# A one-core Flamingo layer stack: the matmul fillers of the slot passes and the last stage left out

## What is computed

```python
x = x + tanh(g_xattn[0]) * L0_xattn(layernorm(x), ctx, ctx, mask)
x = x + tanh(g_ffn[0])   * L0_ffn(layernorm(x))          # relu MLP, 512 wide
x = x + tanh(g_xattn[1]) * L1_xattn(layernorm(x), ctx, ctx)   # one key head
x = x + tanh(g_ffn[1])   * L1_ffn(layernorm(x))          # 16 experts, top 2, and a shared one
x = x + tanh(g_xattn[2]) * L2_xattn(layernorm(x), ctx, ctx)
x = x + tanh(g_ffn[2])   * L2_ffn(layernorm(x))          # 32 experts, top 1
x = x + tanh(g_xattn[3]) * L3_xattn(layernorm(x), ctx)   # slot attention
x = x + tanh(g_ffn[3])   * L3_ffn(layernorm(x), rhs)     # int8 product
```

```python
for _ in range(3):                                   # the slot passes
    q = rmsnorm(slots) @ Wq
    attn = softmax(q @ k.T * scale, axis=slots)      # over the slots
    attn = attn / (attn.sum(axis=keys) + eps)
    slots = gru_cell(attn @ v, slots)                # r, z, n gates
```

## Time and profile before

| | |
|---|---|
| median of 3 runs | 342.53 us (341.97 to 343.16) |
| the profiled execution | 342.59 us |
| its span | 340.3 us |
| mean granted TensorE clock | 0.991 of 2.4 GHz |
| busy: PE | 313.1 us, 92% of the span |
| busy: DVE | 223.9 us, 66% |
| busy: ACT | 132.9 us, 39% |
| busy: POOL | 57.1 us, 17% |

### The profile page before, as it was taken

How to read it: one execution, slowest core, us unless ns; L and a number is a source line. 1 busy time by engine, 2 the same in 40 slices (tenths; PEclk the granted TensorE clock), 3 DMA queues, 4 the chain that set the end, 5 groups by cost and what they waited for, 6 DMA issues and landing times.

```text
span 340.3 us, 5504 instructions
## 1 busy us (share of the span) xinstructions
PE 313.1 (92%) x2029; PEld 190.5 (56%) x2045; DVE 223.9 (66%) x634; ACT 132.9 (39%) x281; POOL 57.1 (17%) x107
## 2 busy tenths in 40 slices
PE   8889999996898999999999998999999988889993
PEld 4453544762435456774568434578677874766441
DVE  4982842678453776478888393543446658899995
ACT  1344263232546352027212716413243544656200
POOL 7231030344002022021000302020210410111220
PEclk9999999998999999999999999999999999999998
DMA  7960000012000000000000000000000000000002
GB/s 187 328 277 0 2 2 0 0 43 94 2 0 2 0 2 0 0 3 0 0 0 2 3 0 2 0 2 1 2 0 2 0 0 3 0 0 2 0 1 62
DMA packets 6958, 8.70 MB, mean 26 GB/s; under 512 B 3067, under 2 KB 5781, under 8 KB 6677
## 3 DMA queue, kind: packets, MB, share of 16 engines
q1 hardware_dynamic: 6933, 8.37, 7.2%
HBM read 7.84 MB, written 0.52 MB: 25 GB/s over the span
## 4 chain that ended last, share of the span: by engine, by line
PE 64%; DVE 23%; ACT 9%; issue 2%; POOL 1%; DVEq 0%; ACTq 0%
PE psum L846 58%; DVE mx L1537 5%; ACT wide L1232 5%; DVE wide L1700 2%; ACT wide L1343 2%; PE psum L937 2%; DVE xn L1717 1%; DVE wide L1707 1%; DVE wide L1706 1%; DVE xn_t L1716 1%; DVE xn L1410 1%; DVE stats L1401 1%; PE psum L1023 1%; PE psum L975 1%; DVE nmax L1671 1%
## 5 line engine op out<-in xcount | busy, mean ns | idle before, releaser
L1537 DVE TENSOR_REDUCE mx<-psum 128x4 f32<-128x308 f32 x96 | 38.6, 472 | 12.4 <-PE psum L846 12.3
L1232 ACT ACTIVATE wide<-psum 128x512 f32<-128x512 f32 x72 | 36.7, 618 | 13.8 <-PE psum L846 13.5
L846 PE MATMUL psum<-xn_t,w_ffn 128*128 128x512 f32 (+1 forms) x88 | 41.6, 597 | 0.0
L1232 ACT ACTIVATE q<-psum 128x512 f32<-128x512 f32 (+1 forms) x36 | 21.2, 594 | 44.0 <-PE psum L846 38.7
L789 POOL TENSOR_SCALAR nw<-mv 128x2 f32<-128x2 f32 x32 | 7.0, 220 | 169.8 <-DVE mv L1404 169.7
L846 PE MATMUL psum<-halves 128*128 128x512 bf16 x111 | 27.9, 386 | 0.5 <-issue 0.2
L846 PE MATMUL psum<-wide 78*128 78x386 f32 (+1 forms) x69 | 25.2, 505 | 3.3 <-DVE wide L1688 2.1
L846 PE MATMUL psum<-xn_t,early 128*128 128x512 f32 x52 | 26.7, 601 | 0.3
L846 PEld LDWEIGHTS psum<-early,wide 128*128 128x128 f32 x192 | 24.0, 192 | 3.2 <-issue 2.0
L1410 DVE TENSOR_SCALAR xn<-x,mv,nw 128x128 f32<-128x128 f32 x64 | 19.1, 343 | 9.6 <-POOL nw L790 9.4
L846 PEld LDWEIGHTS psum<-w_ffn,wide 128*128 128x128 f32 (+1 forms) x176 | 22.3, 191 | 5.3 <-issue 3.7
(11 more groups left out here) (222 smaller groups left out, 503.7 us busy)
## 6 DMA issues: line engine op xcount, KB each, us to landing
w_ffn<-in_ffn SPq DMA_DIRECT2D x1, 2088.5 KB, 12.6
early<-in_ffn SPq DMA_DIRECT2D x1, 1104.0 KB, 5.0
w_attn<-in_attn SPq DMA_DIRECT2D x1, 640.0 KB, 8.0
w_attn<-in_attn SPq DMA_DIRECT2D x2, 288.0 KB, 6.2
x<-in_x SPq DMA_DIRECT2D x2, 256.0 KB, 3.6
early<-in_ffn SPq DMA_DIRECT2D x1, 512.0 KB, 7.0
out<-x SPq DMA_DIRECT2D x2, 256.0 KB, 2.3
rows<-in_rows SPq DMA_DIRECT2D x1, 468.0 KB, 5.9
```

Of the source, the lines that this page charges most:

```text
L846: return nc.tensor.matmul(out_, lhs, rhs, start=start, stop=stop, **kw)
L1232: A.activation(dst, banks.bank(*name)[0:rows_, 0:cols_], fn, **kw).then_inc(drained["act"], 1)
L1537: last = V.tensor_reduce(mx[:, b, t, lane_heads(g)], banks.bank("max", layer, b, t, g)[:, 0:GK].rearrange("p (h k) -> p h k", k=CTX), AX.X ...
```

## The change

```diff
 FILLER = 0.22
-FILL_FROM = 6.0
+FILL_FROM, FILL_UNTIL = 6.0, 280.0
 WARM_UP = 13
...
         if st.engine == "pe":
             units = units_of(st.phase, st.half, st.args)
-            if at > FILL_FROM:
+            if FILL_FROM < at < FILL_UNTIL:
                 (bank, earlier), since = banks.first_free(drained)
                 idle = at - max(free["pe"], since) - FILLER
                 if idle >= FILLER:
```

## The result

Without the fillers the kernel takes 345.82 us (median of 4 runs, 344.97 to 346.12) where the one before takes 342.69 beside it: 3.13 us more, ratio 1.0093 (95% interval 1.0079 to 1.0107). I had forecast 344.2 us, so 1.7 us more. The direction was right, and the measured change is nearly twice (1.84 times) the forecast one.

The account below looks back on a forecast made before the run. From 279 to 334 us DVE was taken as nearly full, PE's share partly filler. Removal 0, first fall 1.2 and last stage 0.5 sum to 1.7 us: 344.2 us, 8-in-10 range 342.9 to 345.9.

Parts of the forecast that it names:

- The removal itself: Dropping nine groups, 93 filler matmuls, due from 280 us on: no real step waits for them, gain 0.
- the rival of steps held back: Steps released before their fillers finish, chiefly at 332.38, would start sooner: at most 1.9 us faster, 340.6; chance 0.03.
- the gap after 284.71: Slot passes: PE idle 3.34 us from the update matmuls' end to the transposes at 288.05; clock falls here.
- The last stage: Half clock from about 320 us; two groups of four matmuls at 332.38 and 335.13 lose 0.25 each, 0.5 us together.
- The transposes there: Last stage, at 328.38 and 332.60: slower at half clock, but fitting into the slack before DVE takes their results.
- the slower ones at 288.68: Four slot transposes, forecast at 288.05: 0.44 us longer, ending 289.12 when ACT is just done (289.22), so covered.
- the term for what the first fall costs: Path work after 289.85 at half clock: bounds 0 and 1.7 us, taken as 1.2.
- 2.29 us of feeding on the path: After 289.85: eight products, eight matmuls of the gate's hidden part and four transposes, whose feeding doubles at half clock.
- further falls: Rival: second half-clock stretch in the third pass, about 315 us, at most 1.7, taken as 1.1: 345.3 us; chance 0.26.
- the gap of 2.0 us: Around 313.10 to 315.12, left empty by seven fillers; named as the place most in danger of a further fall.
- The rule on long gaps: Long idle gaps between matmul bursts halve the clock; by it one fall in the slot passes and no more.
- price for throttled time by the share of the clock that is gone: Half the throttled length: 10 us for about 320 to 340 us; as the full-price rival 354 us, chance 0.01.

Follow-up runs that it names:

- the kernel without the twelve: Kernel before, minus eight fillers ahead of and four behind the slots' transposes of pass 1, half 1: 344.80 us against 342.55, ratio 1.0068.
- without the eight: Kernel before, minus only the eight fillers ahead of the transposes of pass 1, half 1: 344.29 us against 342.55, ratio 1.0055.
- with the twelve thin: Kernel before, its twelve fillers around the transposes of pass 1, half 1 made 64 columns wide instead of 512: 344.70 us against 342.73, ratio 1.0056.
- all four groups gone: Kernel before, minus only the 13 fillers of the four small groups (2, 2, 2 and 7): 343.41 us against 342.55, ratio 1.0039.
- a part of them: Two kernels, each against the one before: minus the seven ahead of pass 2, half 1's update matmuls, 342.84 us; minus the three groups of two, 342.99 us.
- the kernel without the four behind the transposes: Kernel before, minus only the four fillers behind the transposes of pass 1, half 1: 344.02 us against 342.60, ratio 1.0038.
- the one without the twos: Kernel before, minus only the three groups of two fillers in the slot passes: 342.99 us against 342.60, ratio 1.0007.
- ten fillers: Kernel before plus five fillers at 77.6 us and five ahead of the transposes at 80.8 us: 340.75 us against 342.73, ratio 0.9944.

## Why the prediction was right and where it was wrong

**Right.** The removal itself gains nothing: every step that waited for DVE or ACT before still does, and the rival of steps held back did not come; PE still starts 0.14 us after its releaser (at 290.54, behind ACT's end at 290.41). The clock falls in the gap after 284.71 (+0.62), between 286 and 290 us as said (288.57), and again in the last stage. Its price is paid by the products, the hidden part and the transposes on the chain, and feeding doubles. The last stage was put at 0.5 us; alone it measured 0.36, in the profile 0.20 for each of two groups where I had 0.25. In the changed kernel's profile 0.15 for the update matmuls comes on top, which I had not counted. The transposes there and the slower ones at 288.68 were covered, as worked out, but for 0.07 us at ACT.

**Wrong: the length of the first stretch.** The step that failed is the term for what the first fall costs. It was bounded at "3.41 / 2 = 1.7, if PE works on the path through all of them", with the length taken from the one fall that the trace before showed. I took 1.2. It measured 2.23 in the changed kernel's profile, 1.95 in the profile of the kernel without the twelve, and 2.25 as the difference of that kernel's median. The stretch lasted 6.83 us in all four kernels' profiles in which it began in the empty time (the changed one, without the twelve, without the eight, with the twelve thin). In the changed kernel all 2.29 us of feeding on the path (that sum was right) lay in it. I had written that an early fall "leaves the stretch with so little work that a second may follow at half clock", and still kept 1.7 as the end; by that sentence the end should have been the whole 2.3 us. With 2.2 in place of 1.2 the same sum gives 345.2 us.

**Half right: further falls.** I held them for a rival at 0.26 with 1.1 us. The experiments show that they come in some executions (4 of 12 with all four groups gone, 2 of 11 and 2 of 12 with a part of them) and with all four groups gone the median is 0.86 us higher. The executions that have one lie 1.2 to 4.6 us over the median of before; the only one that a profile shows cost 1.2 us. It came not in the gap of 2.0 us, as I thought, but in a stretch with idle times of 0.4 and 0.7 us. In the changed kernel they carry little, if anything: its profile has 38.0 us at half clock and no further fall, and by their mean clocks the four executions have 37.8, 38.5, 38.5 and 32.2 us, with no room for another 3.4 beside the same three stretches. So the 0.86 may not be added to 2.25 + 0.36. What is left between the 2.78 us of the profile and the 3.13 of the medians, 0.35, can be the length of the stretch at 80 us, long in about half of the executions before and by the clocks in at least three of these four; that is an estimate and no run separates it.

**Two rules against the trace.** The rule on long gaps (the Trainium skill, TensorE: Matmul & The Clock Gate, why this matters for your kernels) named the right place, the 3.34 us. Taken as the only condition it failed: the kernel without the four behind the transposes has no gap over 1.61 us there and falls, and so does the one without the twos, in which the idle times are 0.44 and 0.66. The Trainium skill's price for throttled time by the share of the clock that is gone (same page, section Terms) holds for the first stretch only as an upper end (6.83 / 2 = 3.4, measured 2.2) and fails for the last: 19.59 us at half clock cost 0.36.

**Not priced at all:** the stretch at 80 us, which both kernels have. I used it as a yardstick for the clock and didn't ask what it costs: 2.0 us in the medians, more than my whole forecast.

## What to carry to other kernels

A filler is worth what the real work right behind it loses at half clock: twelve fillers ahead of 2.3 us of path matmuls were worth 2.25 us, 68 ahead of eight small matmuls 0.36. Groups that guard the same stretch share one worth: eight alone were worth 1.7, four alone 1.4. Look for places where the granted clock falls before dense work on the critical path, not for where PE is idle longest, and put fillers there even if every bank seems taken, into one that is freed early and overwritten next. Judge such a kernel by many executions and the mean clock of each, since one profile can show the fall missing.

## What the runs showed that I had not expected

The half-clock stretch ahead of the kernel's end came in two lengths. Where it lasted 3.41 us, PE was busy throughout it: seven times, five of them at 80 us and two in the slot passes (without the four, without the twos). Where it lasted 6.83 us, PE stood idle for 0.4 to 2.0 us of it: ten times, six at 80 us and four in the slot passes. Eight fillers of 512 columns and four transposes right before it did not keep the clock up when 1.2 us were empty behind them. And ten fillers, 2.2 us of discarded matmuls, made the kernel 2.0 us faster than before.
